# A hybrid layer on one core: from stage by stage to batch by batch, with the next batch's selective scan in the block of this batch's attention

## The chip, the core and the metric

The kernel runs on one core of a Trainium2 chip. A core has five engines with a queue of instructions each: PE (TensorE, matrix products into PSUM; PEld are its weight loads), DVE (VectorE), ACT (ScalarE), POOL (GpSimd) and SP (SyncE, which here issues every DMA). An engine runs its own queue in order; between engines there are only semaphores. The metric is the time of one execution in microseconds: 1411.6 (median of three runs, 1411.15 to 1412.57).

## The reference

x has 4 batches of 1024 positions with 128 channels. In each of four parts a layernorm goes ahead and the input is added back.

```
x = x + attn_a(layernorm(x))   # gate, depthwise convolution, selective scan
x = x + ffn(layernorm(x))      # dense FFN plus 2 of 8 experts, chosen per batch
x = x + attn_b(layernorm(x))   # gated retention of 16 heads x 8, then softmax attention
x = x + ffn(layernorm(x))      # the same weights again

# attn_a, inner loop over 1024 positions, 16 states n per channel:
h = exp(dt_t[..., None] * A) * h + (dt_t * u_t)[..., None] * B_t[:, None, :]
y = einsum('bdn,bn->bd', h, C_t)
# attn_b, after the retention gave Hseq:
Q, K = l2norm(lin(Hseq)), l2norm(lin(Hseq)); V = lin(x)
attn = softmax(einsum('bhqd,bhkd->bhqk', Q, K) * softplus(temp))
# ffn
main = gelu(x @ W1m + b1m) @ W2m + b2m
top_vals, top_idx = top_k(softmax(mean(x, 1) @ w_gate + b_gate), 2)
out = a * main + (1 - a) * sum_k gate_k * expert_k(x)
```

No batch needs another: every mean, scan and softmax stays within its batch.

## The kernel before, in words

The program is a row of blocks, and each block handles all 4 batches before the next begins. At a block's end all five engines meet at a barrier, so nothing of a block runs beside the next one. The blocks: constants; input layernorms; convolution and inputs of the scan (`scan_inputs`); the scan (`selective_scan`); the first FFN (`ffn`); retention (`retention`); queries and keys (`queries_and_keys`); attention (`attention`); the second FFN; the store. Channels lie on the 128 partitions and time along the free dimension. x stays in SBUF (`x_t`, 128 x 4 x 1024).

Within a block the order is written out by hand. A loop over batches has a body in which the tail of batch b and the head of batch b + 1 stand interleaved (`pipelined`, `there`, and the tables `STEPS` and `NEXT_STEPS` of `ffn`). Counting semaphores (`Count`) guard each buffer.

**The scan.** For each batch there are 16 states n. PE spreads row n of B over 128 partitions (`spread_b`, into one of two `drive_ps`) and row n of C (`spread_c`). ACT makes exp(dt A_n) (`decay`) and copies the spread C to SBUF (`c_rep`). DVE multiplies the spread B by dt u (`drive`, L635) and runs the recurrence over 1024 positions (`scan`, L642), two states at a time: scan, scan, drive, drive. POOL multiplies state by C (`hc`, L685) and PE adds the 16 products in PSUM by an identity product (`add_state`). The same block splits the weights of the 8 experts into two float16 parts, two experts per batch (`SPLITS = (3, 11)`). For an expert SP loads `w_raw`, ACT scales it (`enlarge`, L602) and rounds the high part (`high_part`, L607), POOL forms the rest (`low_part`, L677) and SP stores it. SP's queue holds, per expert, the two loads, a wait for `w_low`, and the store; the loads of the next expert are behind that wait. ACT's `enlarge` waits for the loads.

**The FFN.** 12 chunks of 128 hidden channels per batch (dense and two experts) pass through PE, ACT (gelu, high part), DVE (low part) and PE again, two chunks apart. y is written once per batch (L1006).

**Retention, queries and keys.** Retention runs 8 scans of 1024 positions per batch, in pairs (L1270), with POOL products behind them. Queries and keys are projected by tokens, normalised (L1476) and turned back.

**Attention.** Per batch 4 groups of 4 heads; in each group 16 steps (2 halves of the queries x 8 chunks of 128 keys), so 64 steps v per batch. In a step PE makes two pairs of score products (L1574: 32 rows deep, 512 columns, each pair fills a 128x1024 PSUM buffer), ACT takes the exponential of each buffer (L1612), and PE multiplies the values of step v - 2 by the four heads' exponentials (L1584). There are three score buffers of two PSUM banks and two output banks: all eight. At the end of a group the outputs and denominators are copied, moved across partitions by DMAs, inverted and multiplied. In the loop the projection of a batch waits in the next batch's 15th step, and `take_values` and the DMAs `stack` of the next batch's first groups are issued ahead.

## Time and profile before

| | us |
|---|---|
| median of three runs | 1411.6 |
| the profiled execution | 1415.0 |
| its span | 1413.2 |
| load and input layernorms | 0 to 29 |
| inputs of the scan | 29 to 96 |
| the scan | 96 to 346 |
| first FFN | 346 to 503 |
| retention | 503 to 665.4 |
| queries and keys | 665.4 to 729 |
| attention | 729 to 1243.5 |
| second FFN | 1243.5 to 1400.5 |
| store | 1400.5 to 1413.2 |

Over the span PE is busy 79%, ACT 70%, DVE 59% and POOL 23%; the mean granted clock of PE is 0.92. No engine is at its limit everywhere, so the table by stage has to be read before any share of the whole.

### The profile page before, as it was taken

The numbers are of one execution on the slowest core, as the hardware profiler recorded it, in microseconds if no ns is written. First come the engines' busy times: TensorE is split into PE (matmuls) and PEld (weight loads), VectorE is DVE, ScalarE is ACT, GpSimd is POOL, SyncE is SP. The second block draws the span as 40 slices with busy tenths as digits, with TensorE's granted clock in tenths as the row PEclk, the third lists the DMA queues.
The fourth block names the chain that finished last, engine by engine and source line by source line (L and its number), as shares of the span: only waits on it lengthen the run. The fifth ranks groups of instructions, "written<-read, shape, count | busy, mean of one in ns | idle before, by whom it ended". The sixth has DMA issues, their size and how long they took to land. (4 is left out here: it accounts for less than half of the span.)

```text
span 1413.2 us, 18871 instructions
## 1 busy us (share of the span) xinstructions
PE 1121.0 (79%) x5854; PEld 404.7 (29%) x5854; DVE 835.6 (59%) x1017; ACT 990.6 (70%) x1057; POOL 325.5 (23%) x194
## 2 busy tenths in 40 slices
PE   5748787776899956774539998898999889869996
PEld 3213333332444422321531111111111111124443
DVE  5879998996566559995850432324143232456664
ACT  3767665653788821222439999999999999848885
POOL 3127676765011025654000000000000000011110
PEclk8769999998999979898759999999999999969999
DMA  2000001000100000000010111111011111000001
GB/s 72 0 16 30 30 34 55 30 30 30 31 30 30 30 24 0 0 0 8 0 32 4 35 32 23 22 23 29 19 35 29 23 22 23 14 32 31 30 30 60
DMA packets 24182, 36.28 MB, mean 26 GB/s; under 512 B 7362, under 2 KB 11970, under 8 KB 24130
## 3 DMA queue, kind: packets, MB, share of 16 engines
q1 hardware_dynamic: 24130, 35.71, 9.3%
q8 instruction: 18, 0.29, 0.1%
q14 instruction: 34, 0.28, 0.1%
HBM read 16.82 MB, written 6.29 MB: 16 GB/s over the span
## 5 line engine op out<-in xcount | busy, mean ns | idle before, releaser
L1612 ACT ACTIVATE att_prob<-att_s_ps 128x1024 f32<-128x1024 f32 x512 | 470.8, 1436 | 11.0 <-PE att_s_ps L1574 11.0
L1584 PE MATMUL att_o_ps<-att_prob,att_va 128*32 128x512 f32 x2048 | 277.8, 616 | 2.0 <-ACT att_prob L1612 2.0
L1574 PE MATMUL att_s_ps<-att_q_st,att_k_st 32*128 32x512 f16 x1024 | 194.2, 393 | 49.7 <-ACT att_prob L1612 12.2
L685 POOL TENSOR_TENSOR scan_hc<-scan_state,scan_c_rep 128x1024 f32<-128x1024 f32 x64 | 151.9, 2391 | 71.1 <-DVE scan_state L642 70.8
L1637 DVE RECIPROCAL hv_h_seq<-hv_h_seq 32x1024 f32<-32x1024 f32 (+1 forms) x20 | 105.3, 5265 | 84.3 <-DMA hv_h_seq<-hv_h_seq 84.3
L787 POOL TENSOR_TENSOR ffn_veps<-ffn_mv,all_eps 128x4 f32<-128x4 f32 x16 | 9.1, 569 | 605.4 <-DVE ffn_mv L944 605.4
L642 DVE TENSOR_TENSOR_SCAN scan_state<-scan_decay,scan_drive_ps 128x1024 f32<-128x1024 f32 x64 | 142.9, 2270 | 0.3 <-ACT scan_decay L615 0.3
L1574 PEld LDWEIGHTS att_s_ps<-att_q_st,att_k_st 32*128 32x128 f16 x1024 | 47.0, 91 | 334.7 <-ACT att_prob L1612 315.6
L1651 DVE COPY hv_h_seq<-att_o_ps 128x512 f32<-128x512 f32 x32 | 22.1, 691 | 200.4 <-PE att_o_ps L1584 200.4
L282 PE MATMUL scan_y_ps<-scan_hc,all_ident 128*128 128x512 f32 x256 | 127.5, 622 | 8.6 <-DVE scan_y_sb L661 6.2
L619 ACT ACTIVATE scan_c_rep<-scan_c_ps 128x1024 f32<-128x1024 f32 x64 | 65.5, 1023 | 79.3 <-PE scan_c_ps L282 79.1
L1012 DVE SCALAR_TENSOR_TENSOR ffn_hid_lo<-ffn_hid,ffn_share,ffn_hid_hi 128x1024 f16<-128x1024 f32 x64 | 82.0, 1283 | 48.9 <-ACT ffn_hid_hi L920 48.3
L1318 POOL TENSOR_TENSOR ret_qm<-ret_mem,ret_q_sb 128x1024 f32<-128x1024 f32 x32 | 74.6, 2351 | 64.0 <-DVE ret_mem L1270 61.0
L916 ACT ACTIVATE ffn_hid<-ffn_h_ps,ffn_be 128x1024 f32<-128x1024 f32 x64 | 71.1, 1112 | 21.7 <-PE ffn_h_ps L292 18.6
L635 DVE TENSOR_TENSOR scan_drive_ps<-scan_drive_ps,ssm_du_t 128x1024 f32<-128x1024 f32 x64 | 77.7, 1220 | 13.8 <-PE scan_drive_ps L282 13.5
L282 PE MATMUL scan_drive_ps<-ssm_bc,ssm_sel 96*128 (+1 forms) x128 | 41.6, 408 | 48.1 <-DVE scan_state L642 37.6
L292 PE MATMUL ffn_o_ps<-ffn_hid_hi,ffn_w_sel 128*128 128x512 f16 x256 | 76.0, 379 | 2.2 <-DVE ffn_hid_lo L1012 2.2
L920 ACT ACTIVATE ffn_hid_hi<-ffn_hid,ffn_share 128x1024 f16<-128x1024 f32 x64 | 73.5, 1149 | 4.8
L292 PE MATMUL ffn_h_ps<-ffn_z_hi,ffn_w_sel 128*128 (+1 forms) x256 | 76.2, 379 | 0.0
L615 ACT ACTIVATE scan_decay<-scan_dt_b,scan_a_neg 128x1024 f32<-128x1024 f32 x64 | 73.0, 1140 | 0.1
L1270 DVE TENSOR_TENSOR_SCAN ret_mem<-ret_g_sb,ret_kv_ps 128x1024 f32<-128x1024 f32 x32 | 71.2, 2268 | 0.0
L1012 DVE SCALAR_TENSOR_TENSOR ffn_hid_lo<-ffn_hid,all_blend,ffn_hid_hi 128x1024 f16<-128x1024 f32 x32 | 42.9, 1341 | 44.3 <-ACT ffn_hid_hi L920 44.3
(216 smaller groups left out, 1536.8 us busy)
## 6 DMA issues: line engine op xcount, KB each, us to landing
ffn_w_sel<-w_split SPq DMA_DIRECT2D x16, 512.0 KB, 3.2
w_split<-scan_w_parts SPq DMA_DIRECT2D x8, 512.0 KB, 2.9
att_q_st<-hv_part SPq DMA_DIRECT2D x64, 64.0 KB, 2.1
att_k_st<-hv_part SPq DMA_DIRECT2D x64, 64.0 KB, 2.1
hv_h_seq<-hv_h_seq SPq DMA_DIRECT2D x96, 32.0 KB
ln_x_half<-in_x SPq DMA_DIRECT2D x8, 256.0 KB, 2.9
scan_w_raw<-in_w1e SPq DMA_DIRECT2D x8, 256.0 KB, 3.0
scan_w_raw<-in_w2e SPq DMA_DIRECT2D x8, 256.0 KB, 3.3
```

The lines of the kernel that those rows point to most:

```text
L282: last = pe.matmul(out[:, h], w, rhs[:, h], start=start, stop=stop)
L292: last = pe.matmul(out[:, h], w, x[:, h], start=start and i == 0, stop=stop and i == len(parts) - 1)
L635: dve.tensor_tensor(drive_ps[n % 2][:, :], drive_ps[n % 2][:, :], t.du_t[:, b + n // NS, :], ALU.mult).then_inc(driven.sem, 1)
L642: dve.tensor_tensor_scan(state[:, k % 2, :], decay[:, k % 4, :], drive_ps[k % 2][:, :], 0.0, ALU.mult, ALU.add).then_inc(scanned.sem, 1)
L685: pool.tensor_tensor(hc[:, n % 4, :], state[:, n % 2, :], c_rep[:, n % 4, :], ALU.mult).then_inc(weighed.sem, 1)
L920: act.activation(hid_hi[:, m % 3, :], hid[:, m % 2, :], ACT.Copy, scale=weight_of_expert(k)).then_inc(casted.sem, 1)
L1012: dve.scalar_tensor_tensor(hid_lo[:, m % 3, :], hid[:, m % 2, :], weight_of_expert(m % M // FC), hid_hi[:, m % 3, :], ALU.mult, ALU.subtra ...
L1318: pool.tensor_tensor(qm[:, n, :], mem[:, n % 2, :], q_sb[:, :], ALU.mult).then_inc(weighed.sem, 1)
L1574: last = pe.matmul(s_ps[n % 3][:, i, :], k_st[rows, g % 2, kc * P:(kc + 1) * P], q_st[rows, g % 2, HALVES[half]], start=True, stop=True)
L1584: last = pe.matmul(o_ps[half][32 * j:32 * j + 32, :], va[:, g % 2, kc, j, :], prob[:, u % RING, j, :], start=kc == 0, stop=kc == KC - 1)
L1612: act.activation(prob[:, u % RING, 2 * pair:2 * pair + 2, :], s_ps[n % 3][:, :, :], ACT.Exp).then_inc(exped.sem, 1)
L1637: dve.reciprocal(den[mine, cols], den[mine, cols]).then_inc(recips.sem, 1)
```

## The change

The blocks now go: constants, input layernorms, inputs of the scan (each for all batches, as before), the scan of batch 0, and then for each batch b four blocks: an FFN, retention, queries and keys, attention. The FFN of round b handles two jobs, the first FFN of batch b and the second FFN of batch b - 1 (one job in round 0), and a last FFN block has batch 3 alone. The attention block of batch b also holds the scan of batch b + 1. In all 22 blocks instead of 10.

- **Scan in the attention block.** It runs in 32 steps k (16 states x 2 halves of 512 positions), placed at steps v = 2 + 7k // 4 of the attention. Per step PE spreads B and C (512 columns each, one bank each), ACT makes one decay of 128x512, DVE does three operations of 128x512 (drive, scan, product with C), and POOL adds the product to y in SBUF. The second half's scan starts from the last column of the first.
- **PSUM.** The two banks of the spreads come from the score buffers: two instead of three. The order of a step becomes scores(v, 0), values(v - 2), scores(v, 1), spreads.
- **The block's end.** Nothing of the next batch stands beside it. The four groups' outputs are inverted together, on 128 partitions, in four pieces of 256 columns, after the end of the scan's output.
- **The scan of batch 0** has all 8 experts: `SPLITS = (0, 2, 4, 6, 8, 10, 12, 14)`. SP's queue is otherwise as it was.
- **Constants.** The weights of retention, queries and keys and the output are loaded and split in the first block.
- **Semaphores** are cleared by POOL at each block's end.

```diff
-        SPLITS = (3, 11)
+        SPLITS = (0, 2, 4, 6, 8, 10, 12, 14)
...
+                for k in range(E):
+                    sp.wait_ge(w_scaled.sem, w_scaled.before(k, 0, 1))
+                    sp.dma_start(w_raw[:, 0, :], t.dram["w1e"][k]).then_inc(w_loaded, 16)
+                    sp.dma_start(w_raw[:, 1, :], t.dram["w2e"][k]).then_inc(w_loaded, 16)
+                    sp.wait_ge(w_low.sem, w_low.at(k))
+                    sp.dma_start(t.dram["w_split"][k],
+                                 w_parts[:, :, :, :].rearrange("p w h f -> p (w h f)")).then_inc(w_stored, 16)
...
-        s_ps = [q.ps(f"s_ps{k}", [P, 2, HALF]) for k in range(3)]
+        s_ps = [q.ps(f"s_ps{k}", [P, 2, HALF]) for k in range(2)]
         o_ps = [q.ps(f"o_ps{k}", [P, HALF]) for k in range(2)]
+        b_ps, c_ps = (q.ps(n, [P, HALF]) for n in ("b_ps", "c_ps"))
...
+                def spread(k):
+                    n, h = divmod(k, 2)
+                    pe.wait_ge(scanned.sem, scanned.before(k, 0, 1))
+                    pe.matmul(b_ps[:, :], t.sel[:, n, :], t.bc[:, following, HALVES[h]], start=True,
+                              stop=True).then_inc(b_spread.sem, 1)
+                    pe.wait_ge(weighed.sem, weighed.before(k, 0, 1))
+                    pe.matmul(c_ps[:, :], t.sel[:, NS + n, :], t.bc[:, following, HALVES[h]], start=True,
+                              stop=True).then_inc(c_spread.sem, 1)
...
+                    scores(v, 0)
+                    if v >= 2:
+                        values(v - 2)
+                    scores(v, 1)
+                    for k in steps_at(v):
+                        spread(k)
...
+                def scan_step(k):
+                    n, h = divmod(k, 2)
+                    dve.wait_ge(b_spread.sem, b_spread.at(k))
+                    dve.tensor_tensor(b_ps[:, :], b_ps[:, :], t.du_t[:, following, HALVES[h]],
+                                      ALU.mult).then_inc(driven.sem, 1)
...
+                    dve.tensor_tensor_scan(state[:, k % 2, :], decay[:, k % 4, :], b_ps[:, :], first, ALU.mult,
+                                           ALU.add).then_inc(scanned.sem, 1)
...
+                    dve.tensor_tensor(y[:, HALVES[h]] if n == 0 else hc[:, k % 3, :], state[:, k % 2, :], c_ps[:, :],
+                                      ALU.mult).then_inc(weighed.sem, 1)
...
-            selective_scan(t)
-        ffn(t, "ffn1")
...
+        for b in range(B):
+            ffn(t, f"ffn{b}", [b] if b == 0 else [b, b - 1])
+            with Stage(nc, f"hv{b}") as s:
+                t.h_seq = s.sb("h_seq", [P, T])
+                retention(t, b)
+                queries_and_keys(t, b)
+            attention(t, b)
+        ffn(t, f"ffn{B}", [B - 1])
```

ACT's queue in the scan from one `enlarge` of an expert (`scan_w_large`) on, before:

```order
L602 ACTIVATE scan_w_large<-scan_w_raw 128x1024
L614 REGISTER_ALU
L615 ACTIVATE scan_decay<-scan_dt_b,scan_a_neg 128x1024
L619 ACTIVATE scan_c_rep<-scan_c_ps 128x1024
L605 REGISTER_ALU
L606 REGISTER_ALU
L607 ACTIVATE scan_w_parts<-scan_w_large 128x2x512
L614 REGISTER_ALU
L615 ACTIVATE scan_decay<-scan_dt_b,scan_a_neg 128x1024
L619 ACTIVATE scan_c_rep<-scan_c_ps 128x1024
```

The same queue in the scan of batch 0 now:

```order
L650 ACTIVATE scan_w_large<-scan_w_raw 128x1024
L659 ACTIVATE scan_decay<-all_dt_t,all_a_neg 128x1024
L663 ACTIVATE scan_c_rep<-scan_c_ps 128x1024
L655 ACTIVATE scan_w_parts<-scan_w_large 128x2x512
L659 ACTIVATE scan_decay<-all_dt_t,all_a_neg 128x1024
L663 ACTIVATE scan_c_rep<-scan_c_ps 128x1024
L650 ACTIVATE scan_w_large<-scan_w_raw 128x1024
```

The next `enlarge` comes two states later now; before it came eight states later, so between two of them stood eight pairs of a decay and a copy of C.

PE's queue in one step of attention (`att_s_ps` are scores, `att_o_ps` values), before:

```order
L1568 REGISTER_ALU
L1574 MATMUL att_s_ps<-att_q_st,att_k_st 128x512 x2
L1568 REGISTER_ALU
L1574 MATMUL att_s_ps<-att_q_st,att_k_st 128x512 x2
L1584 MATMUL att_o_ps<-att_prob,att_va 32x512 x4
```

And now, in two steps, of which the first has a step of the scan (`att_b_ps`, `att_c_ps`):

```order
L1533 MATMUL att_s_ps<-att_q_st,att_k_st 128x512 x2
L1544 MATMUL att_o_ps<-att_prob,att_va 32x512 x4
L1533 MATMUL att_s_ps<-att_q_st,att_k_st 128x512 x2
L1551 MATMUL att_b_ps<-all_bc,all_sel 128x512
L1554 MATMUL att_c_ps<-all_bc,all_sel 128x512
L1533 MATMUL att_s_ps<-att_q_st,att_k_st 128x512 x2
L1544 MATMUL att_o_ps<-att_prob,att_va 32x512 x4
L1533 MATMUL att_s_ps<-att_q_st,att_k_st 128x512 x4
```

The values moved in between the two pairs of scores, and the two spreads stand ahead of the next step's first pair.

## Rows read from the trace of the kernel before

**Rows 1.** Windows by stage: stretch, length, busy PE, PEld, DVE, ACT, POOL; clock, DMA

```profile
96.00:346.00 250.00, 193.55 (x528) 77.00 (x528) 230.22 (x140) 154.49 (x153) 170.50 (x73) 0.93 0.11 36
346.00:503.00 157.00, 140.50 (x664) 65.50 (x664) 96.53 (x201) 120.80 (x127) 24.30 (x20) 0.95 0.08 27
503.00:665.40 162.40, 105.06 (x552) 44.19 (x552) 135.81 (x172) 33.15 (x38) 84.09 (x48) 0.86 0.02 5
665.40:729.00 63.60, 31.64 (x192) 30.41 (x192) 46.82 (x53) 26.80 (x34) 0.00 (x0) 0.73 0.01 4
729.00:1243.50 514.50, 449.66 (x3094) 92.07 (x3094) 157.20 (x94) 475.94 (x516) 1.38 (x1) 0.96 0.12 25
```

**Rows 2.** Timeline of the scan's end: start, length, engine, line, idle before

```profile
325.88 2.42 DVE L635 TENSOR_TENSOR scan_drive_ps<-scan_drive_ps,ssm_du_t 128x1024 f32<-128x1024 f32 x2
...
328.50 2.13 POOL L677 TENSOR_TENSOR scan_w_parts<-scan_w_large,scan_w_parts 128x1024 f16<-128x1024 f32 x1
330.59 4.64 POOL L685 TENSOR_TENSOR scan_hc<-scan_state,scan_c_rep 128x1024 f32<-128x1024 f32 x2
...
335.45 1.06 ACT L602 ACTIVATE scan_w_large<-scan_w_raw 128x1024 f32<-128x1024 f32 x1 [6.93 <-DMA scan_w_raw<-in_w2m]
```

**Rows 3.** The page's costliest groups: exponentials of attention, scans, decays

```profile
L1612 ACT ACTIVATE att_prob<-att_s_ps 128x1024 f32<-128x1024 f32 x512 | 470.8, 1436 | 11.0 <-PE att_s_ps L1574 11.0
...
L642 DVE TENSOR_TENSOR_SCAN scan_state<-scan_decay,scan_drive_ps 128x1024 f32<-128x1024 f32 x64 | 142.9, 2270 | 0.3 <-ACT scan_decay L615 0.3
...
L615 ACT ACTIVATE scan_decay<-scan_dt_b,scan_a_neg 128x1024 f32<-128x1024 f32 x64 | 73.0, 1140 | 0.1
```

**Rows 4.** Timeline of attention, from its first exponentials

```profile
739.61 5.61 ACT L1612 ACTIVATE att_prob<-att_s_ps 128x1024 f32<-128x1024 f32 x6
...
768.29 0.39 PE L1574 MATMUL att_s_ps<-att_q_st,att_k_st 32*128 32x512 f16 x4
768.61 1.07 PE L1584 MATMUL att_o_ps<-att_prob,att_va 128*32 128x512 f32 x8
768.80 3.77 ACT L1612 ACTIVATE att_prob<-att_s_ps 128x1024 f32<-128x1024 f32 x4 [1.04 <-PE att_s_ps L1574]
769.61 0.65 PE L1574 MATMUL att_s_ps<-att_q_st,att_k_st 32*128 32x512 f16 x4
```

**Rows 5.** Timeline of attention's end and the next block's first copies

```profile
1223.57 6.37 ACT L1612 ACTIVATE att_prob<-att_s_ps 128x1024 f32<-128x1024 f32 x6
...
1231.91 5.29 SPq L1687 DMA_DIRECT2D hv_h_seq<-hv_h_seq  x8
1235.90 3.35 DVE L1637 RECIPROCAL hv_h_seq<-hv_h_seq 32x512 f32<-32x512 f32 x1 [4.08 <-DMA hv_h_seq<-hv_h_seq]
...
1243.87 1.15 ACT L893 ACTIVATE ffn_x_half<-all_x_t 128x512 f32<-128x512 f32 x2 [13.93 <-PEq L808]
```

**Rows 6.** The line that writes y: first, third and last batch of the first FFN

```profile
L1006 DVE TENSOR_SCALAR ffn_y<-ffn_o_ps,ffn_bias x1: 1279/1279/1279, 399.1 to 399.1; 128x1024 f32<-128x1024 f32 x1
L1006 DVE TENSOR_SCALAR ffn_y<-ffn_o_ps,ffn_bias x1: 1284/1284/1284, 468.8 to 468.8; 128x1024 f32<-128x1024 f32 x1
L1006 DVE TENSOR_SCALAR ffn_y<-ffn_o_ps,ffn_bias x1: 1284/1284/1284, 499.1 to 499.1; 128x1024 f32<-128x1024 f32 x1
```

**Rows 7.** Timeline of retention: its weights, its first and last pairs of scans

```profile
509.17 1.76 DVE L1254 SCALAR_TENSOR_TENSOR ret_w_lo<-ret_w_all,ret_w_hi 128x1536 f16<-128x1536 f32 x1 [0.91 <-ACT ret_w_hi L1206]
...
524.89 4.46 DVE L1270 TENSOR_TENSOR_SCAN ret_mem<-ret_g_sb,ret_kv_ps 128x1024 f32<-128x1024 f32 x2
...
646.29 4.46 DVE L1270 TENSOR_TENSOR_SCAN ret_mem<-ret_g_sb,ret_kv_ps 128x1024 f32<-128x1024 f32 x2
...
653.51 4.46 DVE L1270 TENSOR_TENSOR_SCAN ret_mem<-ret_g_sb,ret_kv_ps 128x1024 f32<-128x1024 f32 x2
```

**Rows 8.** Timeline of queries and keys: the first vector of batches 1 and 2

```profile
692.70 1.23 DVE L1476 TENSOR_TENSOR qk_unit<-qk_raw,qk_rt 128x1024 f32<-128x1024 f32 x1
...
705.87 1.23 DVE L1476 TENSOR_TENSOR qk_unit<-qk_raw,qk_rt 128x1024 f32<-128x1024 f32 x1
```

More of the change, by code:

```diff
@@ L78, in __enter__ @@
     def __enter__(self):
+        self.sems = []
         return self
     def __exit__(self, *a):
+        nums = sorted(sem.num for sem in self.sems)
+        for first in (n for n in nums if n - 1 not in nums):
+            end = next(n for n in range(first, first + len(nums) + 1) if n not in nums)
+            self.nc.gpsimd.sem_clear(range(first, end))
         return self.ctx.__exit__(*a)
@@ L467, in _, with pipelined, there @@
                     pool.tensor_tensor(t.du_t[:, b, :], t.dt_t[:, b, :], t.u_t[:, b, :], ALU.mult)
-def pipelined(eng, first, per, body):
+def pipelined(jobs, first, per, body):
     for n in range(first):
         body(0, n)
-    with eng.Fori(0, B - 1) as b:
+    for i in range(jobs):
         for n in range(first, first + per):
-            body(b, n)
-    for n in range(first, first + per):
-        body(B - 1, n)
-def there(b, n, per):
-    return n < per or not isinstance(b, int) or b < B - 1
+            body(i, n)
+def there(i, n, per, jobs):
+    return n < per or i < jobs - 1
 def selective_scan(t):
@@ L624, in _ @@
-                enlarge(B, 0)
-                high_part(B, 0, t.dense)
+                for n in range(NS):
+                    act.wait_ge(scanned.sem, scanned.before(0, n, 4))
+                    act.activation(decay[:, n % 4, :], t.dt_t[:, 0, :], ACT.Exp,
+                                   scale=t.a_neg[:, n:n + 1]).then_inc(decayed.sem, 1)
+                    act.wait_ge(c_spread.sem, c_spread.at(0, n))
+                    act.wait_ge(weighed.sem, weighed.before(0, n, 4))
+                    act.activation(c_rep[:, n % 4, :], c_ps[:, :], ACT.Copy).then_inc(c_copied.sem, 1)
+                    if n in SPLITS:
+                        enlarge(SPLITS.index(n))
+                    if n - 1 in SPLITS:
+                        high_part(SPLITS.index(n - 1), w_parts)
@@ L627, in _ @@
+                enlarge(E)
+                high_part(E, t.dense)
             @block.vector
@@ L765, in _ @@
             def _(sp):
-                with sp.Fori(0, B) as b:
+                for b in range(N):
                     sp.wait_ge(gate_steps.sem, gate_steps.at(b, 2))
@@ L928, in _ @@
                 shares(0)
-                with act.Fori(0, B - 1) as b:
-                    body(b, False)
-                body(B - 1, True)
+                for b in range(N):
+                    body(b, b == N - 1)
             @block.vector
@@ L1028, in _, with retention @@
                 body(0, 1)
[L1029 removed]
+                for b in range(N):
                     for m in range(LAG, M + LAG):
                         body(b, m)
[L1032 to L1036 removed]
+def retention(t, batch):
     nc, d = t.nc, t.dram
     SUM_AT = 7
[L1049 removed]
+    with Stage(nc, f"ret{batch}") as q:
         x_half = q.sb("x_half", [P, 2, HALF])
@@ L1598, in _, with scores @@
-                pe.wait_ge(exped.sem, exped.at(B - 1, G * U * 2 - 1))
-                project(B, 0)
+                def scores(v, pair):
+                    g, u = divmod(v, U)
+                    half, kc = divmod(u, KC)
+                    pe.wait_ge(exped.sem, exped.before(0, 2 * v + pair, 2))
+                    for i in range(2):
+                        rows = slice(32 * (2 * pair + i), 32 * (2 * pair + i) + 32)
+                        last = pe.matmul(s_ps[pair][:, i, :], k_st[rows, g % 2, kc * P:(kc + 1) * P],
+                                         q_st[rows, g % 2, HALVES[half]], start=True, stop=True)
+                    last.then_inc(scored.sem, 1)
@@ new lines, in values @@
+                def values(v):
+                    g, u = divmod(v, U)
+                    half, kc = divmod(u, KC)
+                    if kc == 0:
+                        pe.wait_ge(out_done.sem, out_done.before(0, g * 2 + half, 2))
+                    pe.wait_ge(exped.sem, exped.at(0, 2 * v + 1))
+                    for j in range(GH):
+                        last = pe.matmul(o_ps[half][32 * j:32 * j + 32, :], va[:, g % 2, kc, j, :],
+                                         prob[:, v % RING, j, :], start=kc == 0, stop=kc == KC - 1)
+                    last.then_inc(used.sem, 1)
```

610 lines of the change are left out of this document (286 added, 324 removed).

## The prediction, on record before the changed kernel ran

> **What bounds the kernel now.** First read the windows by stage [rows 1]. They show a different bound in each. In the scan DVE is busy 230.2 of 250.0 us: 62.5 us per batch, DVE-bound. In attention ACT is busy 475.9 of 514.5 and DVE only 157.2: there DVE, POOL and some PE time are free, and a scan of 56 us of DVE per batch would fit in. The FFN, retention, and queries and keys have no engine that is full, since their batches overlap only in part. Then the page: 512 exponentials take 470.8 us, 0.92 us each, with 11.0 us idle ahead of them [rows 3]. Six alone take 5.61 us [rows 4]: five starts 0.92 apart and a last one of 1.02. An exponential ends after its successor has started, and what waits for its end loses that. Third, the timelines show what a stage costs at its ends, where one batch alone is in flight. That is the number this change multiplies: what was filled once for four batches is now filled four or five times.
>
> **Scan: what goes and what is left.** 250.0 us become the scan of batch 0 alone. Without its weights it would take about 62.5 plus some 5 of filling. But eight experts now pass in 16 states, and their chain is closed. After POOL's rest of an expert begins at 328.50, ACT's next scaling begins at 335.45, 6.95 later: 2.13 of POOL, then the two loads, which SP issues only then, and their landing. The scaling takes 1.06 [rows 2]. Behind it in ACT's queue stands the next decay (1.14 [rows 3]). DVE scans that state (2.27), multiplies two drives (2.42), scans the next state (2.27), POOL multiplies it (2.32, half of the pair's 4.64), and only then comes the next rest. Sum: 6.95 + 1.06 + 1.14 + 2.27 + 2.42 + 2.27 + 2.32 + 0.2 of semaphores = 18.6 us for two states, where DVE needs 7.0. Before, eight states lay between two experts and the load was long there. Seven such rounds are 130. Ahead of them 5.4 (decay, copy, first load and scaling), behind them 17 (1.14 + 2.26 + 2.35, then 2.13 + 4.8 + 1.06 + 1.06 + 2.13 for the last expert and the dense weights; the scan's own end lies beside that). 153 us: **-97**. Bounds: 68 (the chain hidden) to 165.
> The load's leg in this round is 4.8 us, from the end of POOL's rest to the start of the scaling. The Trainium skill, DMA: Bandwidth & Descriptors, gives a fixed cost of about 2.0 us and 436 bytes per ns; for 256 KB and two issues that would be an estimate of 3.2, and the scan 13 us shorter. The trace has the longer one, and the sum above keeps it.
>
> **FFN: +53.** y is written at 399.1, 468.8 and 499.1 for the batches 1, 3, 4 [rows 6]: 34.85 per batch with the next one's layernorm and gate interleaved, 30.3 without. One job alone is 157.0 - 69.7 - 30.3 - 4.5 = 52.5 us, two jobs 87.3. 2 x 52.5 + 3 x 87.3 = 366.9 against 314.
>
> **Retention: +50.** One batch alone: first pair of scans 524.89 - 503.0 = 21.9 after the start, less 2.5 for the weights' split that is gone (DVE's 1.76 and its wait of 0.91) [rows 7], then three intervals of 7.2 (646.29 to 653.51), then 11.9 from the last pair to the end at 665.4. 53.2 x 4 = 213 against 162.4.
>
> **Queries and keys: +16.** The interval between batches is 13.2 (692.70 to 705.87) [rows 8]. One alone is 63.6 - 3 x 13.2 = 24.0, less 3.1 for the temperature and 1.1 for the copy of h, both gone: 19.8 x 4 = 79.
>
> **Attention: +151.** Three parts.
> Its start: from 729.0 to the first exponential at 739.61 [rows 4] is 10.6. The 8 DMAs of the first stack, the first scores and the table load stand in it. Less 0.4 for one DMA: 10.2, four times now. The first steps run with PE slower: 1.5.
> Its body: PE makes two pairs of scores in 0.39 us when nothing holds them (768.29), and the exponential starts 0.51 after the issue (768.80). The values follow the scores by 0.32 (768.61) and hold the next scores for 1.00 (769.61) [rows 4]. With two buffers, pair 1 of step v may start when the exponential of pair 1 of step v - 1 has ended, but it stands behind values(v - 2). The longest circle: pair 0, then 0.31 + 1.00 to pair 1, 0.51 to its exponential, 0.92 to the next one (pair 0 of step v + 1), which ends 1.02 after its start and lets pair 0 of step v + 2 go after 0.05. 3.81 us for two steps: 1.905 per step, where ACT alone needs 2 x 0.92 = 1.84 (and three buffers give it that). 64 x 1.905 = 121.9. A decay of 128x512 is not in the trace. The nearest are the copies of 128x512 from SBUF, two in 1.15 [rows 5], and half of a 1.14 decay: 0.53 to 0.57. Since ACT has only 0.07 of slack a step, 32 decays add 32 x 0.53 = 17. The spreads add 0.45 of PE per scan step, within PE's slack. Only where two scan steps are one v apart (8 of 32) must PE wait for DVE's product, for about 0.25: +2. So 141 with a scan and 122 without. The nearest bounds are ACT alone (134.5) and one more 0.5 to 1.5 us at each of the 96 scan steps.
> Its end: the last exponential ends at 1229.94, the copy of the outputs at 1231.82 (4.08 before 1235.90), the next block's first copy starts at 1243.87 [rows 5]: 13.5. Now DVE first finishes the scan's output: after the copy (1.9 from the last exponential) four operations of 128x512 (2.9), the wait for a product of about 1.2 to 1.9, two additions. That is 8.6. Only then the four inversions. The trace has 3.35 for 512 columns of 32 partitions; I take time by columns, so 4 x (1.7 + 0.35) = 8.2, then the projection 1.5 to 1.9 and an addition: 19.4. In the last batch the last moves set the start of the second half (5.3 of issue plus landing: 9.2 after the last exponential): 15.4.
> 3 x (10.2 + 1.5 + 141 + 19.4) + (10.2 + 1.5 + 122 + 15.4) = 3 x 172.1 + 149.1 = 665.4, against 514.5. The scans themselves cost this stage 3 x 23, the lost overlap and the two buffers the rest.
>
> **Small terms.** The first block now holds 10 DMAs, the split of 1536 columns (1.76 on DVE [rows 7], as much again at most on ACT) and table loads: +7, bounds 4 to 10. Clears of semaphores at 22 block ends: no row. The way from one block to the next stands in the terms above; for the clears +4, bounds 0 to 20.
>
> **Sum.** -97 + 53 + 50 + 16 + 151 + 7 + 4 = +184. Span 1413.2 + 184 = 1597. The profiled execution took 1.8 more than its span, and the median of the runs lies 3.4 under the profiled execution: **1596 us**. That is 13% slower. The 187 us of three scans were to vanish. 90 of them are paid again as the weights' chain, 119 is paid to the fills of three kinds of block, and attention grows by a third.
>
> **Rivals.**
> 1. *The scan inside attention holds PE's queue* (24%). PE waits in order for DVE at the spreads: b for the last scan, c for the last product. If DVE's three operations with their semaphores (0.69 + 1.18 + 0.69 and more, by halves of the durations of 1024) or POOL's additions take longer than the 1.75 steps between them, every score behind waits. For it: b_ps and c_ps are single, and ACT has hardly any slack. Against it: 2.7 us of DVE against 3.7 us between scan steps. Price 0.5 to 1.5 us at 96 scan steps: 1644 to 1740.
> The Trainium skill, TensorEngine Tiling, Key Properties, says that a change of the tiling mode drains TensorE; the scan adds two changes at each spread. At the 0.39 of a score product per drain that is an estimate of 75 us and this rival's time; the trace shows values only 0.32 behind the scores, which speaks for a smaller price.
> 2. *The weights' chain does not hold the scan* (6%): then the scan is 68 and the whole 1511. For it: the store and the loads are 3 us each in the trace. Against it: the order in SP's queue and ACT's.
> 3. *Not slower* (1%). If an engine that is done with its block went on into the next, the batches would overlap across blocks and the fills would vanish: 119 us of the three kinds, and some 20 of each attention's 30 us of ends, 199 in all: 1397. It decides from 184 us of recovered fill. Against it: ACT sat idle 13.93 us ahead of 1243.87, through the whole end of attention [rows 5], so it had no way into the next block.
>
> **Numbers.** Forecast 68% (1545 to 1644), rival 1 24%, rival 2 6%, rival 3 1%, and 1% for the rest. The forecast's own range has ACT-bound steps and shorter ends below (-51) and more PE stalls and dearer clears above. The range that holds 8 in 10 is 1545 to 1665. A difference of 0.2% is about what the measurement can tell from none. Faster by over 0.2%: 1%. Within 0.2%: 1%. Slower: 98%.
>
> **What would show it.** In the new profile: ACT's `enlarge` eight times some 18.6 us apart, with an idle wait on the DMA of `w_raw` ahead of each; FFN blocks of 52 and 87 us; retention 53; queries and keys 20; attention about 172 and 149 from start to start, its steps 1.9 us apart in the last batch and 2.2 on average with a scan; DVE inverting after the last addition of the scan's output. Wrong would be: steps of 1.84 in the last batch (two buffers would be enough), experts 7 us apart, steps over 2.5 us with a scan, or a block that starts while the one before still runs.

## The result and the profile after

| | us |
|---|---|
| before, median of 4 runs | 1412.09 (1411.15 to 1413.03) |
| changed, median of 4 runs | 1593.46 (1591.0 to 1595.44) |
| ratio | 1.1284 (95% interval 1.1263 to 1.1305) |
| forecast | 1596, range 1545 to 1665 |

The profiled execution took 1595.03, its span 1593.2. The kernel is 12.8% slower. First the windows by stage, one for each kind of block; columns as in [rows 1].

```profile
103.40:267.40 164.00, 68.03 (x132) 23.37 (x132) 58.52 (x35) 50.68 (x51) 56.30 (x26) 0.66 0.16 55
267.40:317.30 49.90, 38.15 (x166) 17.57 (x166) 24.45 (x50) 30.70 (x32) 4.87 (x6) 0.84 0.07 22
317.30:372.90 55.60, 33.15 (x138) 12.80 (x138) 34.12 (x42) 9.02 (x10) 20.98 (x12) 0.71 0.00 0
372.90:392.20 19.30, 9.30 (x48) 8.74 (x48) 11.84 (x13) 6.06 (x7) 0.00 (x0) 0.68 0.00 0
392.20:563.50 171.30, 139.80 (x840) 28.61 (x840) 104.50 (x124) 140.65 (x161) 39.67 (x31) 0.90 0.09 19
563.50:648.90 85.40, 72.53 (x332) 33.68 (x332) 48.67 (x101) 60.00 (x63) 11.33 (x10) 0.91 0.08 26
1385.70:1530.40 144.70, 115.45 (x772) 23.18 (x772) 16.13 (x22) 121.22 (x129) 1.38 (x1) 0.92 0.10 22
```

In order: the scan of batch 0, an FFN with one job, retention, queries and keys, attention with a scan, an FFN with two jobs, the last attention. In the 164 us of the scan no engine is busy for more than 68, and DVE for 58.5, where [rows 1] had it at 230 of 250. The terms of the forecast beside these lengths:

| term | forecast | measured | from |
|---|---|---|---|
| first block | +7 | +7 | 103.4 - 96 |
| scan | -97 | -86 | 164.0 - 250.0 |
| FFN | +53 | +42 | 2 x 49.9 + 3 x 85.4 - 314 = 356 - 314 |
| retention | +50 | +59 | some 55.4 x 4 - 162.4 |
| queries and keys | +16 | +14 | some 19.4 x 4 - 63.6 |
| attention | +151 | +143 | 171.3 + 171.1 + 171.1 + 144.5 - 514.5 |
| clears of semaphores | +4 | 0 | what is left beside the others |

The sum is 180 where 184 was forecast. It is closer than its terms: they are off by up to 11, in both directions. Each length goes from one block's start to the next one's, so what a clear costs would lie in the terms above; it is looked at by itself further below.

**The scan.** One round of the weights' chain, from the timelines of DVE, POOL, ACT and PE, one after the other (start, length, engine, line, idle before):

```profile
152.08 1.21 DVE L679 TENSOR_TENSOR scan_drive_ps<-scan_drive_ps,all_du_t 128x1024 f32<-128x1024 f32 x1
155.73 1.23 DVE L679 TENSOR_TENSOR scan_drive_ps<-scan_drive_ps,all_du_t 128x1024 f32<-128x1024 f32 x1 [2.44 <-PE scan_drive_ps L341]
...
161.53 2.12 POOL L721 TENSOR_TENSOR scan_w_parts<-scan_w_large,scan_w_parts 128x1024 f16<-128x1024 f32 x1
...
147.69 1.06 ACT L650 ACTIVATE scan_w_large<-scan_w_raw 128x1024 f32<-128x1024 f32 x1 [14.76 <-DMA scan_w_raw<-in_w2e]
168.37 1.06 ACT L650 ACTIVATE scan_w_large<-scan_w_raw 128x1024 f32<-128x1024 f32 x1 [14.78 <-DMA scan_w_raw<-in_w2e]
...
150.75 1.03 PE L341 MATMUL scan_c_ps<-all_bc,all_sel 96*128 96x512 bf16 x2 [11.51 <-ACT scan_c_rep L663]
151.58 3.62 PE L341 MATMUL scan_y_ps<-scan_hc,all_ident 128*128 128x512 f32 x4
155.00 0.70 PE L341 MATMUL scan_drive_ps<-all_bc,all_sel 96*128 96x512 bf16 x2
155.53 0.59 PE L341 MATMUL scan_c_ps<-all_bc,all_sel 96*128 96x512 bf16 x2
155.96 1.88 PE L341 MATMUL scan_y_ps<-scan_hc,all_ident 128*128 128x512 f32 x4
```

The chain is the one that was written down: POOL's rest ends at 163.65, the scaling starts at 168.37, 4.72 later (forecast 4.8), and ACT sits idle 14.8 us until its load lands. But this round is 20.7, not 18.6 (20.2 on the mean). The surplus is in "DVE multiplies two drives (2.42)": the second drive waits 2.44 for its spread (155.00). That spread stands in PE's queue behind four additions to y that take 3.62. PE had been idle for 11.5 us before them, and the granted clock of the stretch is 0.66, a mean of the two levels (1.2 and 2.4 GHz): two spreads of the same form take 1.03 at 150.75 and 0.59 at 155.53, and the same four additions take 1.88 at 155.96. So of the 2.44 an estimated 1.7 (3.62 - 1.88) is the lower level, and the other 0.7 is the place in the queue.

**Attention.** The page's group that answers to [rows 3], then the timeline of the first attention block at its two ends:

```profile
L1597 ACT ACTIVATE att_prob<-att_s_ps 128x1024 f32<-128x1024 f32 x512 | 489.7, 1025 | 39.5 <-PE att_s_ps L1533 36.7
```

```profile
399.59 3.77 ACT L1597 ACTIVATE att_prob<-att_s_ps 128x1024 f32<-128x1024 f32 x4 [5.71 <-PE att_s_ps L1533]
403.22 0.74 ACT L1589 ACTIVATE att_decay<-all_dt_t,all_a_neg 128x512 f32<-128x512 f32 x1
403.83 1.04 ACT L1597 ACTIVATE att_prob<-att_s_ps 128x1024 f32<-128x1024 f32 x1
...
539.21 4.76 ACT L1597 ACTIVATE att_prob<-att_s_ps 128x1024 f32<-128x1024 f32 x5
...
551.48 0.75 DVE L1676 SCALAR_TENSOR_TENSOR all_x_t<-att_c_ps,all_vec,all_x_t 128x512 f32<-128x512 f32 x1 [0.79 <-PE att_c_ps L1573]
552.15 1.74 DVE L1626 RECIPROCAL att_den<-att_den 128x256 f32<-128x256 f32 x1
564.07 1.15 ACT L934 ACTIVATE ffn_x_half<-all_x_t 128x512 f32<-128x512 f32 x2 [20.09 <-PEq L851]
```

The last attention block:

```profile
1393.02 4.69 ACT L1597 ACTIVATE att_prob<-att_s_ps 128x1024 f32<-128x1024 f32 x5 [5.66 <-PE att_s_ps L1533]
...
1499.68 15.06 ACT L1597 ACTIVATE att_prob<-att_s_ps 128x1024 f32<-128x1024 f32 x16
...
1530.97 1.15 ACT L934 ACTIVATE ffn_x_half<-all_x_t 128x512 f32<-128x512 f32 x2 [16.23 <-PEq L851]
```

The block starts at 392.3. First exponential 7.3 later; from it to the end of the last one (539.21 + 4.76 = 543.97) 144.4; from there to the block's end at 563.4 another 19.4. The last block has 7.3, 121.7 and 15.6. The forecast had 11.7, 141 and 19.4, and 11.7, 122 and 15.4. A decay takes 0.61 from its start to the next exponential. DVE inverts only after the scan's output (551.48, then 552.15), as forecast.

### The profile page after: what moved, and what is told of

It reads as the page before. It is cut to its first block and busy times, and to the rows that moved or that the text cites. A ratio compares the mean times of both kernels' runs of the same rounds, so it can differ in the third digit from the quotient of the medians.

```text
span 1593.2 us, 16615 instructions
## 1 busy us (share of the span) xinstructions
PE 1127.4 (71%) x5658; PEld 385.4 (24%) x5658; DVE 842.3 (53%) x1213; ACT 957.2 (60%) x1052; POOL 325.0 (20%) x239
## 5 line engine op out<-in xcount | busy, mean ns | idle before, releaser
L1597 ACT ACTIVATE att_prob<-att_s_ps 128x1024 f32<-128x1024 f32 x512 | 489.7, 1025 | 39.5 <-PE att_s_ps L1533 36.7
L1517 POOL TENSOR_TENSOR att_y<-att_y,att_hc 128x512 f32<-128x512 f32 x90 | 114.9, 1276 | 304.1 <-DVE att_hc L1651 304.1
L1638 DVE TENSOR_TENSOR att_b_ps<-att_b_ps,all_du_t 128x512 f32<-128x512 f32 x96 | 66.9, 697 | 139.5 <-PE att_b_ps L1551 139.5
L1621 DVE COPY att_o_sb<-att_o_ps 128x512 f32<-128x512 f32 x32 | 21.9, 685 | 159.6 <-PE att_o_ps L1544 159.6
L957 ACT ACTIVATE ffn_hid<-ffn_h_ps,ffn_be 128x1024 f32<-128x1024 f32 x64 | 71.1, 1110 | 18.3 <-PE ffn_h_ps L351 16.4
L686 DVE TENSOR_TENSOR_SCAN scan_state<-scan_decay,scan_drive_ps 128x1024 f32<-128x1024 f32 x16 | 36.5, 2281 | 79.3 <-issue 67.8
L351 PE MATMUL ffn_h_ps<-ffn_z_hi,ffn_w_sel 128*128 128x512 f16 x256 | 76.2, 379 | 0.0
L650 ACT ACTIVATE scan_w_large<-scan_w_raw 128x1024 f32<-128x1024 f32 x9 | 9.5, 1056 | 110.5 <-DMA scan_w_raw<-in_w2e 101.1
L1589 ACT ACTIVATE att_decay<-all_dt_t,all_a_neg 128x512 f32<-128x512 f32 x96 | 68.8, 717 | 0.0
L842 POOL TENSOR_TENSOR all_x_t<-all_x_t,ffn_y 128x1024 f32<-128x1024 f32 x8 | 21.4, 2671 | 222.8 <-DVE ffn_y L1046 222.8
L1651 DVE TENSOR_TENSOR att_hc<-att_state,att_c_ps 128x512 f32<-128x512 f32 x90 | 61.8, 687 | 3.1
```

Source lines behind the costliest of these rows:

```text
L351: last = pe.matmul(out[:, h], w, x[:, h], start=start and i == 0, stop=stop and i == len(parts) - 1)
L957: act.activation(hid[:, m % 2, :], h_ps[m % 2][:, :], ACT.Gelu_apprx_tanh, bias=b1, scale=1.0 / WS).then_inc(gelued.sem, 1)
L1517: pool.tensor_tensor(y[:, HALVES[h]], y[:, HALVES[h]], hc[:, k % 3, :], ALU.add).then_inc(summed.sem, 1)
L1589: act.activation(decay[:, k % 4, :], t.dt_t[:, following, HALVES[h]], ACT.Exp, scale=t.a_neg[:, n:n + 1]).then_inc(decayed.sem, 1)
L1597: act.activation(prob[:, v % RING, 2 * pair:2 * pair + 2, :], s_ps[pair][:, :, :], ACT.Exp).then_inc(exped.sem, 1)
L1638: dve.tensor_tensor(b_ps[:, :], b_ps[:, :], t.du_t[:, following, HALVES[h]], ALU.mult).then_inc(driven.sem, 1)
```

## The experiments

Each is compared with the kernel before on its own chip. Differences between two variants are taken from their profiled executions or from the ratios.

**1. The loads ahead.** In the scan of batch 0, SP's queue:

```diff
+                load(0)
                 for k in range(E):
-                    # the two loads of expert k
+                    load(k + 1)
                     sp.wait_ge(w_low.sem, w_low.at(k))
                     sp.dma_start(t.dram["w_split"][k], ...)
```

> The changed kernel, with the loads of the next expert issued by SP before it waits for the present one's low part and stores it. Theory (the chain of the weights is closed and the load's leg of 4.7 us stands in it): each of the seven rounds in the scan of batch 0 falls from 20.3 to about 15.7, the last leg to the dense weights by 4.3, so the scan falls from 164 to about 127 and the whole from 1593 to about 1556. Rival (the states themselves, slow on PE at a clock of 0.67, hold the round): the round stays above 19 and the whole above 1582.

Measured: 1562.91, ratio 1.1057 (1.1033 to 1.1080), against 1.1284: 31 us less. One of its scalings:

```profile
169.76 1.06 ACT L652 ACTIVATE scan_w_large<-scan_w_raw 128x1024 f32<-128x1024 f32 x1 [10.29 <-POOL scan_w_parts L723]
```

The scaling now waits for POOL's rest of the expert before, no longer for a load, and a round takes 15.3 to 16.4 (the first one 13.6): 109.4 us for the seven instead of 141.2, 4.5 less each. The load's leg stood in the chain nearly with its full 4.7 us; the rival falls. The whole was expected lower, at 1556: the scan still takes some 133, not 127, since its own last output (DVE's, from 234.75 to 236.03 in this run) now ends after the weights, where both ended together before.

**2. As 1, and two buffers for scaled weights and parts.**

```diff
-        w_parts = s.sb("w_parts", [P, 2, 2, F], F16)
+        w_large = [s.sb(f"w_large{k}", [P, 2, F]) for k in range(2)]
+        w_parts = [s.sb(f"w_parts{k}", [P, 2, 2, F], F16) for k in range(2)]
-                    act.wait_ge(w_low.sem, w_low.before(k, 0, 1))
+                    act.wait_ge(w_low.sem, w_low.before(k, 0, 2))
```

> As loads_ahead, and with two buffers for the scaled weights and two for their parts, so that no expert waits for the one before. Theory (only the closed chain holds the scan of batch 0): DVE's 7.0 us per two states sets the pace, ACT needs 6 and POOL 6.8, PE's clock comes back above 0.9, the scan of batch 0 takes about 78 instead of 164 and the whole about 1507. Rival (POOL, with 4.65 of products and 2.12 of low part per two states, or PE at its low clock then holds it): 95 to 110 for the scan, 1525 to 1540.

Measured: 1518.5, ratio 1.0765 (1.0726 to 1.0804). The scan takes some 90, between the two, and for neither reason: the raw weights still had one buffer, and six of the seven scalings after the second waited 1.0 to 6.8 us for their load. The longest:

```profile
166.24 1.06 ACT L653 ACTIVATE scan_w_large<-scan_w_raw 128x1024 f32<-128x1024 f32 x1 [6.76 <-DMA scan_w_raw<-in_w2e]
```

**3. Two raw buffers too, and a shorter end of attention.** The load goes two experts ahead; in attention the scan's output and the division of the first half move ahead of the last copy:

```diff
-                take_out(G - 1, 1)
                 if following is not None:
                     # the scan's output
                 dve.wait_ge(moved, G * MOVES)
                 divide(0)
+                take_out(G - 1, 1)
```

> The changed kernel with two buffers for raw weights, scaled weights and parts, and the load two experts ahead; and with the scan's output and the division of the first half put ahead of the last copy of the outputs in each attention block. Theory: the scan of batch 0 is bound by DVE and takes about 78 (164 in the changed kernel, 89 with single raw weights), and the end of an attention with a scan falls from 19.4 to the last batch's 15.6: 1593 - 86 - 3 x 3.8 = 1496. Rival (POOL's 6.8 us per two states holds the scan now, and the division delays the last copy by 1 to 2): 1505 to 1515.

Measured: 1502.63, ratio 1.0634 (1.0597 to 1.0671). Its window of the scan:

```profile
103.00:174.70 71.70, 53.01 (x132) 18.19 (x132) 58.53 (x35) 51.10 (x51) 56.18 (x25) 0.88 0.36 125
```

The scan falls to some 72 (it began at 102.3 here): of the 164 us 92 were the weights' chain. DVE is busy the same 58.5 us, and PE's clock came up from 0.66 to 0.88 with nothing changed on PE. The end of attention gave less than expected: 1.1 a block (171.5 to 170.4 from the table load to the next block's first copy) instead of 3.8. At the end of its first attention block:

```profile
450.05 1.02 ACT L1604 ACTIVATE att_prob<-att_s_ps 128x1024 f32<-128x1024 f32 x1 [1.21 <-PE att_s_ps L1540]
451.37 1.02 ACT L1604 ACTIVATE att_prob<-att_s_ps 128x1024 f32<-128x1024 f32 x1 [0.29 <-PE att_s_ps L1540]
469.69 1.15 ACT L941 ACTIVATE ffn_x_half<-all_x_t 128x512 f32<-128x512 f32 x2 [17.29 <-PEq L858]
```

From the last exponential's end (452.39) to the next block (0.6 ahead of 469.69) it is 16.7 instead of 19.4, but the scan's product on PE stands in the last steps now and stops ACT for 1.5 (1.21 and 0.29), and the way from the first to the last exponential grew from 144.4 to 146.1. The first theory was right for the scan, the second, with another place for the loss, for attention.

**4 to 6. Where a scan's 22.7 us (144.4 - 121.7) in attention come from.** These kernels leave work out: 28 of 32 decays, 31 of 32 pairs of spreads, and both. The first edit, then the second:

```diff
                 def decays(k):
+                    if k >= 4:
+                        return
...
-                    dve.wait_ge(decayed.sem, decayed.at(k))
+                    dve.wait_ge(decayed.sem, decayed.at(min(k, 3)))
```

```diff
                     for k in steps_at(v):
-                        spread(k)
+                        if k == 0:
+                            spread(k)
...
-                    dve.wait_ge(b_spread.sem, b_spread.at(k))
+                    dve.wait_ge(b_spread.sem, b_spread.at(0))
```

> The changed kernel, but ACT makes only the first four half decays of each scan inside attention and the later steps use them again (this leaves out 28 of 32 decays, the values of the scans of batches 1 to 3 are not the reference's). Theory (what a scan costs attention is ACT's own time): a body with a scan falls from 144.4 to between 122 and 127, the whole from 1593 to about 1540 (28 x 0.61 x 3 = 51 less). Rival (PE's queue, held by DVE at the spreads, costs it): the bodies stay above 138 and the whole above 1575.

> The changed kernel, but in attention PE spreads B and C only for the first half step of a scan; DVE's later steps work on what stands in the two banks (this leaves out 31 of 32 pairs of spreads, so the scans of batches 1 to 3 are not the reference's). With 28 of 32 decays left out a body went from 144.4 to about 135, not to the forecast's 125. Theory, now corrected (about half of a scan's 22.7 us in attention is PE's time and its waits at the spreads, half ACT's): a body falls by about 11 to 133 and the whole from 1593 to about 1560. Forecast's split (ACT 17 to 19, PE 2): a body falls by 3 and the whole to about 1584.

> The changed kernel without 28 of 32 decays and without 31 of 32 pairs of spreads in each scan inside attention (their values are not the reference's); DVE's and POOL's work stays. Decays alone gave 9.4 us of the 22.7 of a body back, spreads alone 2.7. Theory (ACT's decays and PE's wait at the spreads lie beside each other, so each alone covers for the other): both together give back 20 or more, and the whole is about 1525. Rival (the two add up, and something third, DVE or POOL, costs the remaining 10): about 12 a body, 1557.

| | whole | ratio, interval | first to last exponential with a scan | less |
|---|---|---|---|---|
| changed | 1593.46 | 1.1284 | 144.4 | |
| no decays | 1562.14 | 1.1054 (1.1031 to 1.1077) | 136.2 | 8.2 |
| no spreads | 1582.57 | 1.1192 (1.1155 to 1.1230) | 141.6 (142.6 in the third) | 2.8 |
| neither | 1531.5 | 1.0852 (1.0830 to 1.0873) | 124.8 | 19.6 |

By the rows it is 136.2 and 8.2 without decays, not the 135 and 9.4 that two of the expectations name. Where this column comes from, in the last kernel (398.83 to 519.83 + 3.84):

```profile
398.83 1.94 ACT L1600 ACTIVATE att_prob<-att_s_ps 128x1024 f32<-128x1024 f32 x2 [5.71 <-PE att_s_ps L1533]
...
519.83 3.84 ACT L1600 ACTIVATE att_prob<-att_s_ps 128x1024 f32<-128x1024 f32 x4
```

What PE waits for from 392 to 545, in the first attention block of the changed kernel and then without decays (groups by line: idle before, releaser):

```profile
L1533 PE MATMUL att_s_ps<-att_q_st,att_k_st 32*128 32x512 f16 x256 | 50.5, 403 | 21.3 <-ACT att_prob L1597 10.0 <-DMA att_k_st<-all_part 9.2
L1551 PE MATMUL att_b_ps<-all_bc,all_sel 96*128 96x512 bf16 x32 | 12.9, 403 | 0.0
L1554 PE MATMUL att_c_ps<-all_bc,all_sel 96*128 96x512 bf16 x32 | 12.7, 397 | 1.8 <-DVE att_hc L1651 1.8
```

```profile
L1533 PE MATMUL att_s_ps<-att_q_st,att_k_st 32*128 32x512 f16 x256 | 48.7, 403 | 13.6 <-DMA att_k_st<-all_part 9.2 <-ACT att_prob L1599 3.0
L1551 PE MATMUL att_b_ps<-all_bc,all_sel 96*128 96x512 bf16 x32 | 12.9, 403 | 1.4 <-DVE att_state L1648 1.4
L1554 PE MATMUL att_c_ps<-all_bc,all_sel 96*128 96x512 bf16 x32 | 12.7, 397 | 2.3 <-DVE att_hc L1653 2.3
```

In the changed kernel PE idles 10.0 us for exponentials; without decays only 3.0, and now it waits for DVE at the spreads of B as well (1.4, where it was 0.0). Two paths of nearly one length lie beside each other: ACT's decays, and PE's spreads with their waits for DVE. Each hides behind the other, so one alone gives little back and both together 19.6. My reading after the first of these runs, that half of the price was PE's, fell with the second: the forecast's expectation (a body falls by 3) was right there. The forecast's split, ACT 17 and PE 2, names the longer path rightly, but not how close the other one is.

The Trainium skill, TensorEngine Tiling (Array Packing), Key Properties, has a change of tiling mode drain TensorE. It gives no price; an estimate with a score product per drain was 75 us for the 192 added changes. Taking 31 of 32 pairs of spreads out gives 2.8 a body, 8 in all; where ACT no longer covers them it is 11.4 a body (19.6 - 8.2), 34 in all, with the products themselves in it. The estimate is over double of that, so the traces do not bear it out. Whether some of the 11.4 is a drain they do not show.

**7. Two score buffers in the kernel before.** Three buffers become two, and the order is that of the changed kernel:

```diff
-                            for pair in range(2):
-                                scores(g, u, pair)
+                            scores(g, u, 0)
                             if (g, u) >= (0, 2):
                                 values(*divmod(g * U + u - 2, U))
+                            scores(g, u, 1)
```

> The kernel before with two score buffers instead of three and the changed kernel's order on PE (first pair of scores, values, second pair). The forecast's circle of 1.905 us per step against 1.84 for three buffers: 256 x 0.065 = 17 us more, 1430. Rival (three buffers don't give 1.84 either: 490.3 us from the first to the last exponential over 256 steps is 1.915 already): no difference within 0.3%, 1410 to 1416.

Measured: 1429.44, ratio 1.0117 (1.0089 to 1.0144), 16.5 us more. From the first to the last exponential it is now 507.2 instead of 490.3, 0.066 a step on the mean, which is the number of the forecast's circle. But the pace changed by less: the 512 exponentials take 480.1 us instead of 470.8, 1.875 a step instead of 1.84, where the circle has 1.905. The rest, 7.2 us, is longer waits at some steps (18.2 instead of 11.0 in all), among them 3.2 ahead of each of three exponentials (895.75, 1023.92 and 1151.68) at the projections. The rival took the 1.915 of the kernel before for its pace; it is 1.84 (470.8 over 256) and the 11.0 of [rows 3], and the rest are the loads of ACT's table at the start of batches 1 to 3. The first and the last exponentials with two buffers, the page's group of them, and the group of the table loads in the kernel before:

```profile
736.55 3.77 ACT L1612 ACTIVATE att_prob<-att_s_ps 128x1024 f32<-128x1024 f32 x4
...
1239.86 3.84 ACT L1612 ACTIVATE att_prob<-att_s_ps 128x1024 f32<-128x1024 f32 x4
...
L1612 ACT ACTIVATE att_prob<-att_s_ps 128x1024 f32<-128x1024 f32 x512 | 480.1, 1022 | 18.2 <-PE att_s_ps L1574 18.0
```

```profile
L1612 ACT ACT_TABLE_LOAD x4 | 5.1, 1283 | 15.3 <-PE att_s_ps L1574 15.3
```

**8. FFN blocks of one job.**

```diff
-            ffn(t, f"ffn{b}", [b] if b == 0 else [b, b - 1])
+            ffn(t, f"ffn{b}", [b])
+            if b:
+                ffn(t, f"again{b}", [b - 1])
```

> The changed kernel with each FFN block of two jobs taken apart into two blocks of one job, so three blocks more and not one operation more. Theory (a block costs its fill, whatever it holds): 2 x 49.9 - 85.4 = 14.4 per block, 43 in all, 1636. Rival (the fill is mostly a slow clock after attention's end, not the missing overlap): the second block of a pair runs at a high clock and costs less than 8 more, below 1617.

Measured: 1631.37, ratio 1.1546 (1.1522 to 1.1571), 37 more by the ratios. The two blocks that were one of 85.4:

```profile
561.00:611.00 50.00, 38.43 (x166) 17.73 (x166) 24.68 (x51) 30.92 (x32) 4.61 (x5) 0.84 0.07 22
611.00:661.40 50.40, 39.10 (x166) 17.87 (x166) 24.45 (x50) 29.53 (x31) 4.86 (x6) 0.84 0.07 22
```

Both cost the same and have the same clock, one behind an attention and one behind an FFN; together they take 15.0 more than one block of two jobs. The price is the block's. The three pairs cost 43 to 44 us more by the rows, but the whole only 35 (spans 1628.2 and 1593.2): retention with queries and keys behind them took 5.9 less in three blocks (73.2, 73.3 and 71.0 us at granted clocks of 0.73, 0.73 and 0.78, where the changed kernel has some 74.5 at 0.71 to 0.72), and this run reached its first FFN 2.4 earlier. What raised that clock was not looked into.

**9. Retention and queries and keys batch by batch, in the kernel before.**

```diff
-            retention(t)
-            queries_and_keys(t, s)
+            for b in range(B):
+                t.h_seq, t.v_tok, t.part = h_all[:, b, :], v_all[:, b, :, :], part_all[:, b, :, :, :]
+                retention(t, b)
+                queries_and_keys(t, b)
```

> The kernel before with retention and queries and keys as eight blocks of one batch each, as the changed kernel has them (with its constants in the first block and its clears of semaphores), and everything else as before. Theory (every block costs its fill, wherever it stands): 4 x 55.6 - 162.4 = 60, 4 x 19.3 - 63.6 = 14, and 7 for the first block: 1412 + 81 = 1493. Rival (the fill belongs to the neighbours, after an attention that leaves PE's clock low): under 1475.

Measured: 1496.01, ratio 1.0588 (1.0550 to 1.0627): 83 more. By the rows 75 of them stand in these blocks (301 us from 507.3 to 808.6, against 226); the changed kernel's first block and its clears are in this run too, and it reaches retention 4.3 later. The first of its four pairs of blocks:

```profile
507.30:583.10 75.80, 43.15 (x186) 21.71 (x186) 45.86 (x55) 15.08 (x17) 20.97 (x12) 0.70 0.00 1
```

The others take 75.3, 75.1 and 75.1: 75 us each, as in the changed kernel (55.6 + 19.3).

**10 and 11. Batches in pairs.** The price is per block, so fewer blocks should keep the gain of the scan in attention and pay half the fills:

```diff
-        for b in range(B):
-            ffn(t, f"ffn{b}", [b] if b == 0 else [b, b - 1])
+        for k in range(2):
+            ffn(t, f"ffn{k}", [0, 1] if k == 0 else [2, 3, 0, 1])
...
+            attention(t, k)      # both batches; with k == 0 also the scans of 2 and 3
+        ffn(t, "ffn2", [2, 3])
```

The scan block has batches 0 and 1, four experts each, with the buffers of experiment 3. The exponentials and retention's products lie where the scans' inputs of batches 0 and 1 were. In the middle of an attention block the projection of its first batch stands 11 steps into the second, in the banks of the spreads.

> A version of its own: batches in pairs. Scan of batches 0 and 1 (weights with two buffers of each), then for the pairs (0, 1) and (2, 3) an FFN, retention, queries and keys and an attention, each overlapped within its pair; the first attention block holds the scans of 2 and 3. 13 blocks instead of 22. Theory (a block costs its fill whatever it holds, and a scan in attention 22.7 instead of 62.5): 103 for the start, 133 for two scans, 85.4 + 157 + 85.4 for the FFNs, 2 x (55.6 + 36.2) for retention, 2 x (19.3 + 13.2) for queries and keys, 7.3 + 2 x 144.4 + 15.6 = 312 and 7.3 + 2 x 121.7 + 15.6 = 266 for the attentions, 13 for the store: 1404, 0.6% below the kernel before. Rival (the seam between two batches in one attention, where DVE finishes the scan, divides and adds, stops PE or ACT by 5 or more, and the second scan in 47 steps is too dense): 1415 to 1430.

Measured: 1393.2, ratio 0.9871 (0.9851 to 0.9891), faster than the kernel before by 1.3%. Its windows: the scans, and parts of the attention of batch 0, of batch 1, and of batches 2 and 3.

```profile
103.20:230.60 127.40, 98.32 (x264) 38.76 (x264) 114.61 (x70) 83.53 (x83) 94.37 (x42) 0.92 0.20 71
445.00:585.00 140.00, 125.27 (x813) 26.00 (x810) 93.65 (x110) 137.40 (x159) 38.29 (x30) 0.98 0.10 22
585.00:730.00 145.00, 132.77 (x852) 29.17 (x845) 104.45 (x123) 140.91 (x163) 38.66 (x30) 1.00 0.09 19
1035.00:1278.00 243.00, 220.29 (x1532) 45.02 (x1528) 21.52 (x31) 239.59 (x256) 0.00 (x0) 0.98 0.11 24
```

ACT is busy 137.4 of 140, 140.9 of 145 and 239.6 of 243. From the first to the last exponential the first attention block takes 285.2, no more than twice 144.4, and at the seam ACT waits 1.5 (1.21 ahead of 590.12 and 0.29 ahead of 591.43), so the rival falls. The scans took 127 instead of 133, the first two FFN blocks 84.6 and 153.6 instead of 85.4 and 157.

Then three score buffers in the second attention block, which has no spreads:

> As pairs, but the second attention block, which has no scan and so two banks over, has three score buffers, the order of the kernel before on PE, and the projection of its first batch in one of them at the 15th step of its second. Theory (before_two_scores: two buffers cost 16.8 us over 256 steps, 0.066 a step): 128 x 0.066 = 8 less than pairs, 1385. Rival (the projection inside a score buffer stops the steps and takes it back): 1390 to 1393.

Measured: 1389.68, ratio 0.9815 (0.9792 to 0.9838). In the profiled executions its second attention goes from the first to the last exponential in 237.3 us instead of 243.0:

```profile
1037.62 1.94 ACT L1653 ACTIVATE all_u_t<-att_s_ps 128x1024 f32<-128x1024 f32 x2 [5.65 <-PE att_s_ps L1574]
...
1272.11 2.78 ACT L1653 ACTIVATE all_du_t<-att_s_ps 128x1024 f32<-128x1024 f32 x2
```

That is 5.7 of the 8 expected. The 0.066 a step behind the 8 was a mean with waits in it; the pace alone (0.036 in experiment 7) is worth 4.6 over 128 steps. ACT waits 1.88 once for the projection in a score buffer (ahead of 1184.95), little more than the 1.5 with two buffers. It is the fastest version, 1.8% below the kernel before.

## Why the prediction was right

- **Direction and mechanism: right.** The three vanished scans are paid again by the weights' chain, the fills and attention. Experiment 3's scan shows the chain (92 us of 164), 8 and 9 show the fills, and 10 shows that with the chain open (1502.63) and half the rounds of blocks the sign turns.
- **Scan, -97 forecast, -86 measured.** The chain and its load leg are right. The step that failed is "multiplies two drives (2.42)": in a chain that leaves PE idle for 11 us its additions ran at the lower clock, and the second drive came 2.44 late. Seven rounds took 141 (108.67, the first scaling, to 249.90, the eighth) where 130 were forecast: the whole 11. The prediction's estimate of 3.2 for the load's leg took a figure that the Trainium skill (DMA: Bandwidth & Descriptors, Anatomy of one DMA — SWDGE (gpsimd) path) gives for DMAs issued from GpSimd. Here SP issues them; from issue to landing the two loads take 3.4 and 3.8, and the store's issue stands ahead of them in SP's queue.
- **FFN, +53 forecast, +42 measured.** The terms 52.5 and 87.3 should have been 49.9 and 85.4. They were differences between moments of DVE in a running pipeline. The interval of 30.3 and the end of 3.9 held; what came out shorter is the way to the first y: 51.2 with two jobs where 53.1 was taken, 45.9 with one where 48.6 was left after the 4.5 (34.85 - 30.3). Why the kernel before needs 1.9 more there was not looked into.
- **Retention, +50 forecast, +59 measured.** The step that failed is "three intervals of 7.2": they were 8.0, 7.2 and 8.9, read at POOL's products (the last two below). The parts of the forecast add up to 52.9, not 53.2; the start (19.4) and the end (12.0) held, and the intervals are the 2.5 between 52.9 and some 55.4. Alone in its block a batch leaves PE at a clock of 0.71 (0.86 in [rows 1]), and the products ahead of the last pair take 1.06 for two, where two of the same form take 0.59 earlier in the block (at 350.16):

```profile
354.35 4.65 POOL L1323 TENSOR_TENSOR ret_qm<-ret_mem,ret_q_sb 128x1024 f32<-128x1024 f32 x2 [2.57 <-DVE ret_mem L1276]
363.23 4.63 POOL L1323 TENSOR_TENSOR ret_qm<-ret_mem,ret_q_sb 128x1024 f32<-128x1024 f32 x2 [4.23 <-DVE ret_mem L1276]
...
358.57 1.06 PE L351 MATMUL ret_kv_ps<-ret_z_hi,all_ret_lo 128*128 128x512 f16 x2
```

- **Attention, +151 forecast, +143 measured.** The start was 7.3, not 11.7: ACT loads its table (1.28) before the first scores now, the first four stack DMAs are issued in 2.5 us instead of 3.8, and the 1.5 for slower first steps was not seen beside the body. The body without a scan (122) and both ends (19.4, 15.4) held within 0.3. For the body that is in part luck: its exponentials take 119.9, a pace of 1.87 a step and not the circle's 1.905, and waits of 1.7 in the first steps make up for it. The body with a scan was 144.4, 3.4 over the forecast's 141. The term that was mis-sized is the decay: ACT's part is 19.9 (141.6 without spreads, less 121.7) where 32 x 0.53 = 17 was forecast, since a decay costs ACT 0.61. The spreads add 2.8 where 2 was forecast.
- **Clears of semaphores, +4 forecast.** No run shows a cost. From the FFN to retention's first copy ACT waits 7.52 without them (kernel before) and with them (changed kernel):

```profile
503.67 1.15 ACT L1174 ACTIVATE ret_x_half<-all_x_t 128x512 f32<-128x512 f32 x2 [7.52 <-PEq L1097]
```

```profile
317.92 1.15 ACT L1196 ACTIVATE ret_x_half<-all_x_t 128x512 f32<-128x512 f32 x2 [7.52 <-PEq L1120]
```

- **Rivals.** Rival 1 (1644 to 1740) fell; its mechanism is there with 3 us a body. Rival 2 fell: the chain held the scan with 92 us. Rival 3 fell: no block starts while another runs; ACT sits idle 20.1 us ahead of 564.07, through the end of the first attention.

The errors were +11, -11, +9, -2, -8 and -4, and they cancel. That the sum was right within 4 us is luck beyond its terms; a reader should trust those to some 10 us each.

## What to carry to other kernels

A block between barriers costs its fill each time, here 15 us for an FFN and 25 for a retention with its queries and keys ((301 - 226) / 3); before work is regrouped to hide 62 us behind another engine, count the blocks it adds. A background job that kept its place while the foreground got four times shorter (the weights' split) becomes the chain: see which buffers close it. And of two paths of nearly one length, taking away one shows less than it costs (8.2 and 2.8 here, where both gave 19.6); take away both before saying what a thing costs.
